# Which row chunks SyncE fetches in a graph-attention kernel: the first of every fourth group in place of the last of every fifth

## What is computed

```python
h = jnp.einsum('ni,hif->hnf', x, W)                  # 8 heads of 32
ea = (s_src[:, src] + s_dst[:, dst]).T               # one score per edge and head
ea = jnp.where(ea > 0, ea, NEG_SLOPE * ea)
ea = jnp.exp(ea - segment_max(ea, dst)[dst])
ea = ea / (segment_sum(ea, dst)[dst] + EPS)
out = segment_sum(hn[src] * ea[:, :, None], dst)     # one row of h gathered per edge
```

## Time and profile before

| | us |
|---|---|
| median of 3 runs | 3227.16 (3221.13 to 3239.17) |
| profiled execution | 3236.36 |
| its span | 3235.1 |

### The profile page before, as it was taken

How to read it: one execution, slowest core, us unless ns; L and a number is a source line. 1 busy time by engine, 2 the same in 40 slices (tenths; PEclk the granted TensorE clock), 3 DMA queues, 4 the chain that set the end, 5 groups by cost and what they waited for, 6 DMA issues and landing times.

```text
span 3235.1 us, 48074 instructions
## 1 busy us (share of the span) xinstructions
PE 2639.1 (82%) x11525; PEld 2048.5 (63%) x11525; DVE 2017.3 (62%) x5482; ACT 1553.6 (48%) x3392; POOL 2218.1 (69%) x2172
## 2 busy tenths in 40 slices
PE   8657776889888898888988886654578999999997
PEld 6545555567666666666666664443457878787886
DVE  7445567668777676777767776878455554455322
ACT  5335543545545465554654544433344454544443
POOL 0277777777777777777777777777547667776554
PEclk9879988999999999999999998786789999999999
DMA  8797766566666666666666666566756676666653
GB/s 275 241 305 205 199 167 180 164 172 184 169 176 182 176 181 174 170 180 176 179 176 170 180 166 184 158 176 184 232 152 164 151 162 149 151 134 131 139 100 57
DMA packets 403074, 563.65 MB, mean 174 GB/s; under 512 B 73911, under 2 KB 323820, under 8 KB 402615
## 3 DMA queue, kind: packets, MB, share of 16 engines
q0 software_dynamic: 122976, 296.52, 35.7%
q1 hardware_dynamic: 202487, 174.80, 18.6%
q10 hardware_dynamic: 77255, 88.59, 10.1%
HBM read 402.43 MB, written 169.68 MB: 177 GB/s over the span
## 4 chain that ended last, share of the span: by engine, by line
PE 46%; SPq 12%; issue 10%; DVE 9%; DMA 8%; ACT 7%; POOL 7%; ACTq 1%; DVEq 0%; POOLq 0%
PE bank L1504 15%; SPq L1396 8%; PE bank L2553 7%; PE bank L2566 7%; PE bank L1185 4%; PE bank L1174 3%; POOL out L2644 3%; DMA rows<-table,srcix 2%; POOL rows L1416 2%; SPq L1393 2%; DMA rows<-spare 1%; PE bank L690 1%; DMA spare<-table 1%; PE bank L691 1%; PE bank L1147 1%
## 5 line engine op out<-in xcount | busy, mean ns | idle before, releaser
L1416 POOL DMA_INDIRECT rows<-table,srcix x1522 | 1459.9, 959 | 463.8 <-issue 324.2
L1504 PE MATMUL bank<-rows,onehot 128*128 128x272 f32 x3328 | 920.6, 423 | 56.8 <-ACT fout L1563 52.4
L1563 ACT ACTIVATE fout<-bank 128x272 f32<-128x272 f32 x1659 | 639.0, 397 | 572.0 <-PE bank L1504 525.9
L1504 PEld LDWEIGHTS bank<-rows,onehot 128*128 128x128 f32 x3328 | 660.7, 206 | 239.9 <-ACT fout L1563 77.5
L1660 DVE TENSOR_TENSOR rows<-rows,bank 128x1024 f32<-128x1024 f32 x416 | 484.1, 1214 | 155.8 <-ACT rows L1552 155.5
L2644 POOL DMA_INDIRECT out<-x_y,x_dest x203 | 328.3, 1617 | 260.4 <-DMA out<-x_y,x_dest 168.8
L2553 PE MATMUL bank<-x_int,x_w1c 128*128 128x256 f32 (+1 forms) x1696 | 379.5, 378 | 24.3 <-issue 21.0
L2566 PE MATMUL bank<-e_w,x_ht 128*128 x1624 | 374.6, 384 | 12.2 <-issue 6.7
L2553 PEld LDWEIGHTS bank<-x_int,x_w1c 128*128 128x128 f32 x1696 | 316.8, 194 | 75.0 <-issue 33.1
L2592 ACT ACTIVATE x_ht<-bank,x_b1c 128x256 f32<-128x256 f32 (+1 forms) x424 | 172.8, 462 | 392.6 <-PE bank L2553 392.2
L2566 PEld LDWEIGHTS bank<-e_w,x_ht 128*128 128x128 f32 x1624 | 302.8, 192 | 56.3 <-issue 18.7
(11 more groups left out here) (461 smaller groups left out, 3406.5 us busy)
## 6 DMA issues: line engine op xcount, KB each, us to landing
frag<-fout ACTq DMA_DIRECT2D x104, 544.0 KB
spare<-table SPq DMA_DIRECT2D x1920, 1.1 KB
x_in<-sorted_d SPq DMA_DIRECT2D x97, 260.0 KB
rows<-table,srcix POOLq DMA_INDIRECT x1522
x_b2c<-in_L_ffn_b SPq DMA_DIRECT2D x106, 128.0 KB, 3.5
frag<-in_x ACTq DMA_DIRECT2D x1, 13416.0 KB
table<-hr SPq DMA_DIRECT2D x24, 544.0 KB, 4.1
xs<-in_x SPq DMA_DIRECT2D x24, 512.0 KB, 6.2
```

What stands on the lines that cost most here:

```text
L1416: p.indirect_dma_start(out=B.rows[b][:, j, :], out_offset=None, in_=B.table[:, :], in_offset=bass.IndirectOffsetOnAxis(ap=chunk_columns(B. ...
L1504: pe.matmul(B.banks[2 + c % 3][:, 0:ROW], B.onehot[k % 2][:, j, :], B.rows[k % NR][:, j, :], start=True, stop=True).then_inc(S.sum, 1)
L1563: a.activation(B.fout[k % 2][:, j, :], B.banks[2 + c % 3][:, 0:ROW], ACT.Copy).then_inc(S.ev, 1)
```

## The change

`SPARE_EVERY` goes from 5 to 4, and the groups from 27, 32, ... 97 (15) to 24, 28, ... 96 (19). The chunk is 0 and no longer 15. For each chunk SyncE first passes three empty parts, then issues the 128 rows over 13 parts, and the move is no longer in the last part but at the head of the next one, the first step of loop g-2; it waits for the sum of chunk 0 of group g-3. The three empty parts of the next chunk come right behind it. Rows, register loads and the move itself are as before.

```diff
-SPARE_FROM, SPARE_EVERY = 20, 5
-SPARE_CALLS = 4 * SPARE_EVERY
-SPARE_GROUPS = list(range(SPARE_FROM + SPARE_EVERY + 2, SPLIT - 1, SPARE_EVERY))
-SPARE_CHUNK = CB - 1
+SPARE_FROM, SPARE_EVERY = 17, 4
+SPARE_GROUPS = list(range(SPARE_FROM + SPARE_EVERY + 3, SPLIT - 1, SPARE_EVERY))
+SPARE_CHUNK = 0
...
+    def move(i, g):
+        sp.wait_ge(S.spare, 16 * (P + 1) * (i + 1))
+        ids(i + 1)
+        sp.wait_ge(S.sum, (g - NR) * CB + SPARE_CHUNK + 1)
+        sp.dma_start(B.rows[g % NR][:, SPARE_CHUNK, :], B.spare[:, :]).then_inc(S.moved, 16)
+
+    calls = 4 * SPARE_EVERY - 3
+    rows = [P * t // calls for t in range(calls + 1)]
     sp.wait_ge(S.mixp, 5)
     ids(0)
     yield
     for i, g in enumerate(SPARE_GROUPS):
-        rows = [0] + [P * (t + 1) // SPARE_CALLS for t in range(SPARE_CALLS)]
+        yield from idle(3)
         sp.wait_ge(S.spare, 16 * ((P + 1) * i + 1))
...
-            if hi == P:
-                sp.wait_ge(S.spare, 16 * (P + 1) * (i + 1))
-                ids(i + 1)
-                sp.wait_ge(S.sum, (g - NR) * CB + SPARE_CHUNK + 1)
-                sp.dma_start(B.rows[g % NR][:, SPARE_CHUNK, :], B.spare[:, :]).then_inc(S.moved, 16)
             yield
+        move(i, g)
```

## The result

| | before | after |
|---|---|---|
| median, us | 3224.47 | 3331.11 |
| profiled execution, us | 3236.36 | 3331.2 |
| its span, us | 3235.1 | 3329.9 |

The changed kernel takes 1.0334 times as long (95% interval 1.0312 to 1.0357), 107 us more. The forecast was 3333. Medians in this document are over all executions, but ratios leave out two slow ones at a lower granted clock: one of the fifth experiment (3340.75 us at 0.817) and one of the kernel before beside it (3625.56 us at 0.731).

What follows compares the result with a forecast made beforehand. POOL bounds the kernel before; after, SyncE's 87 us period against POOL's 79.6 puts the move for group 96 at 739 + 17 x 87 = 2218, so 3227 + 106 = 3333 us; range 3220 to 3395.

Steps and rivals of the forecast that it cites:

- POOL sets the pace: Edge stage before the change: 1646 POOL calls at 1.27 us make 2090 of 2106 us; ACT's waits are absorbed.
- Rival 2: Score copy: ACT's waits for the move lie on the path; the earlier move removes 143.5 us, 3084 us; chance 4%.
- the term that carried the sum: SyncE's period for four groups: 87 us against POOL's 79.6, so each move falls 7.4 us further behind.
- first move of the slow stretch: SyncE's move for group 28: goes out at about 739 us, some 5 us after POOL is done with that group.
- Rival 1: Row issues at bare pitch: SyncE keeps up, period 78.8 to 79.6 us, POOL stays the bound, 3222 us; chance 14%.
- The other signs: SyncE's waits for others near zero, POOL waits near 7 us per four groups, ACT's waits on the move above 143.5 us.
- The parts of the period: SyncE per four groups: 66.0 us for the chunk plus 4 x 4.8 us for groups, 85.2 of work; landings 1.8.
- The long row issues: SyncE's issues up to 1.94 us, counted per group; if they went with rows, a period about 1.6 us longer.
- The stock: Row buffers: a score copy less than about 18 us late is absorbed; used up after two periods.
- The +106 us: Edge stage: POOL begins group 98 at 2223.5 in place of 2117.83; what follows moves as a block.
- the last step of the sum: Move for group 96 at 2218 lets POOL go on 5.5 us later, two groups on, at group 98.
- Rival 3: SyncE is the bound and still waits for others, 5.8 us per period: period 93, +208, 3435 us; chance 7%.

Runs made afterwards that it cites:

- the fifth experiment: The changed kernel with each group's two id loads issued by ScalarE and source numbers loaded 32 registers at a time, not 16: 3227.95 us, ratio 1.0007 to the kernel before.

## Why the prediction held, point by point

**POOL sets the pace, ACT's waits don't.** Right. With every fifth group in the new order ACT's 143.5 us of waits for the move are gone and the time stays (0.9992). Rival 2 is out.

**SyncE has no room for a chunk per four groups.** Right, and by the term that carried the sum: period 87 forecast, 86.9 measured; first move of the slow stretch (group 28) 739 forecast, 746.06 measured; last 2218 and 2223.84. Rival 1 is out: its condition was row issues at their bare pitch, without the long ones, and a period of 79.6 us at most; the long ones hold 5.98 us per chunk, as before (next paragraph). Half the issues bring the time back. The other signs came as well: the 123.7 us of real waits before POOL's calls are 7.3 us for each of 17 periods, and ACT's waits on the move rose to 199.3 us.

**The parts of the period.** The sum was good, its parts less so. Forecast: 85.2 us of work and 1.8 of landings; measured 85.8 and 1.1. The long row issues were counted per group, some 1.6 of the 4.8 us that were put down to each. In the changed kernel the issues over 0.3 us hold 5.98 us more than the median per chunk, before it was 5.91: they stayed with the chunk. The rest of what was put down to them, 8.0 us for five groups before, was in part slow register loads (1.434 us at the mean, 1.244 at the median, eight per chunk). ACT's store of last rows does stand beside many of them: 68 of these 157 long issues start within 2 us behind the start of such a store, and hold 4.05 of the 5.98 us; before, 54 of 122. But not each store has one behind it: 52 of 67 do, where before 40 of 65 did. So a store costs more when SyncE issues rows nearly all the time, and a count per group does not carry over. The other long issues stand elsewhere. The rule of the Trainium skill that was weighed there (Perfetto Trace Analysis, section "DMA Instruction — HWDGE (DVE, Sync)": two queues share a descriptor generator) agrees with these counts for the issues near a store, but no run took the stores away.

**The stock.** Right: 18 us. In the changed kernel the score copy of group 32 is 25.3 us late, and the first call two groups on waits 7.52 us in place of 0.30, so 18.0 us were absorbed. For 13 of the 16 fetched groups from 32 to 92 this difference is 18.0 to 18.5 us (13.4, 13.6 and 19.7 for the other three), and the copy of group 96, 18.1 us late, makes no call wait. Wrong was when it is used up: after one period from group 28 and not two, since the move for group 28 came 7 us later than forecast and the next period was 91.8 us.

**The +106 us.** POOL begins group 98 115.7 us later, 10 more than forecast, and the last step of the sum did not happen. By it the move for group 96, at 2218, lets POOL go on 5.5 us later at the first call of group 98. That move was 6 us late, at 2223.84, but the call at 2233.51 has its usual 0.30 us before it, and the score copy of group 96 waited for its own engine:

```profile
2229.83 0.42 ACT L1544 ACTIVATE sc_e<-rows 128x256 f32<-128x256 f32 x1 [0.91 <-ACT fout L1566]
```

The last move behind which POOL waits at the first call two groups on is that for group 92:

```profile
2145.12 0.94 POOL L1419 DMA_INDIRECT rows<-table,srcix  x1 [9.68 <-PE bank L1507]
```

Behind it POOL has waits of 1.63, 3.74 and 2.30 us in groups 94 to 96, which the sum had at nothing. The last of them, before 2201.67, comes right behind a wait of PE for a load of the merges that SyncE issues as well (at 2192.25); that this load caused it is argued from the order, not shown by a run:

```profile
2199.05 1.02 PE L1753 MATMUL bank<-ident,mg_last 128*8 128x128 f32 x4 [10.40 <-DMA mg_first<-frag]
```

What adds up is POOL's own account ahead of group 98: 123.7 us of real waits, less 5.1 for four calls and some 4 for slightly shorter calls, is about 115.

POOL's last gather ends 114.8 us later as well (2372.41 + 0.94 against 2257.63 + 0.95 in the trace of before). Behind it the experts took 956.5 us where the profiled execution of before took 976.6; over the nine profiled kernels this tail, which none of them changes, lies between 956 and 977. So the profiled executions differ by 95 us and the medians by 107. That the medians' tails differ by the missing 8 us is a subtraction, not read from a trace: the match to 2 us is partly luck, the period is not.

**Rival 3.** Not in the changed kernel: no wait for PE or DVE is left but 0.5 us. It is real, though, in the order of before at every fourth group, at 2.3 us per period.

## What to carry to other kernels

Before handing work to an engine that seems free because it only issues DMAs, add up its period: work, waits for its own DMAs, and waits for others; only the last is room, here 5.8 of 99.4 us. 128 single-row issues cost SyncE about 71 us with their register loads and the long ones among them, and save POOL one call of 1.27 us, so such a trade pays only while the room lasts. When an engine is the bound, a step that has nothing to do with the change (here the id loads) is as good to move as any, and where its one blocking step stands in the loop is worth microseconds per round.

## What was not expected of the hardware

A register load does not cost by the value alone: 16 values take 1.24 us, 32 take 2.135 us. If the cost is a straight line through these two, 0.35 us of each load do not depend on the count. And an issue on SyncE's queue that takes 0.225 us at the median took up to 1.73 us within 2 us of ScalarE's stores in the changed kernel. All long issues together hold about 6 us per chunk, with the chunk spread over four groups (5.98) as over five (5.91 in the kernel before); over the eight versions with 128 issues it is 4.9 to 6.1 us, with no order by the number of groups.
